# The recurrence's products, sums and last ratio on another engine, and its keys turned one slice later

## The reference, cut to what matters

```python
x = x + tanh(g_ffn[0])   * ffn0(layernorm(x), W_up, W_gate, W_down)      # silu(up) * gate, 2048 wide
x = x + tanh(g_xattn[1]) * wkv(w, u, k=layernorm(x), v=ctx)

def step(carry, kv_t):                # wkv, scanned over the 256 positions, per channel
    p, q, o = carry
    kt, vt = kv_t
    no = maximum(o, u + kt)
    A = exp(o - no)
    E = exp(u + kt - no)
    y = (A * p + E * vt) / (A * q + E)
    no2 = maximum(w + o, kt)
    A2 = exp(w + o - no2)
    E2 = exp(kt - no2)
    return (A2 * p + E2 * vt, A2 * q + E2, no2), y
```

## Time and profile before

| | |
|---|---|
| median of 3 runs | 3439.24 us (3435.51 to 3440.72) |
| the profiled execution, first to last instruction | 3438.0 us |
| the same beside the median of the runs | 1.2 us less |
| mean granted TensorE clock | 0.944 |
| a pass of the stage (passes 3 to 6) | 53.5 us |
| the stage, from its first matmul to the last L856 | 403.4 to 879.5 us |

### The profile page before, as it was taken

The page is one execution under the profiler, slowest core; times in us unless marked ns, Lnnn a source line. Parts: engine busy times, 40 slices in busy tenths (PEclk is TensorE's granted clock), DMA queues, the critical chain, the costliest instruction groups (busy, mean ns, idle before and its releaser), DMA issues.

```text
span 3438.0 us, 50056 instructions
## 1 busy us (share of the span) xinstructions
PE 2938.0 (85%) x18354; PEld 1708.0 (50%) x18354; DVE 2538.5 (74%) x4602; ACT 1663.7 (48%) x2597; POOL 955.8 (28%) x1357
## 2 busy tenths in 40 slices
PE   4999898884689899677788747999999999988998
PEld 2344566663344444355666523455555455544665
DVE  5699669999766666688888878777777777766333
ACT  3000144444345555248889974444454444455433
POOL 2566100000300000025767775222222222211000
PEclk7999999997799999899899968999999999999999
DMA  7233111212211011110000021000000000021000
GB/s 266 81 92 92 41 56 61 62 50 73 57 26 32 23 26 47 53 38 7 1 1 2 9 93 55 1 7 7 1 7 7 1 7 7 1 65 37 13 18 18
DMA packets 52643, 132.51 MB, mean 39 GB/s; under 512 B 6416, under 2 KB 19536, under 8 KB 51152
## 3 DMA queue, kind: packets, MB, share of 16 engines
q1 hardware_dynamic: 43216, 96.11, 9.2%
q10 hardware_dynamic: 9216, 33.56, 3.2%
HBM read 119.03 MB, written 4.19 MB: 36 GB/s over the span
## 4 chain that ended last, share of the span: by engine, by line
PE 50%; DVE 24%; issue 12%; ACT 10%; POOL 3%; DMA 1%; DVEq 0%; SPq 0%; POOLq 0%; ACTq 0%
PE psum L1106 10%; PE psum L517 8%; ACT area_g L2149 4%; PE psum L2074 4%; PE psum L2604 3%; PE psum L2563 3%; PE psum L668 3%; PE psum L2588 2%; PE psum L2573 2%; PE psum L1955 2%; DVE area_a L1713 2%; PE psum L2095 2%; PE psum L1361 2%; PE psum L1342 2%; DVE xn L2861 1%
## 5 line engine op out<-in xcount | busy, mean ns | idle before, releaser
L2149 ACT ACTIVATE area_g<-area_a 128x2048 bf16<-128x2048 f32 x168 | 334.7, 1997 | 33.3 <-POOL area_a L2018 24.0
L2074 PE MATMUL psum<-area_c,ident_bf 128*128 128x128 bf16 x3328 | 231.1, 234 | 97.6 <-DVE area_c L2183 97.5
L172 POOL TENSOR_TENSOR rstd<-mean_var,eps_col 128x2 f32<-128x2 f32 x65 | 21.3, 327 | 1048.3 <-DVE mean_var L590 565.0
L517 PE MATMUL psum<-area_b,area_g 128*128 128x512 f32 x640 | 279.1, 599 | 3.9 <-DVE x_stream L455 2.4
L2074 PEld LDWEIGHTS psum<-area_c,ident_bf 128*128 128x128 bf16 x3328 | 216.2, 106 | 122.9 <-DVE area_c L2183 116.0
L2563 PE MATMUL psum<-area_b,stage 128*128 128x512 f32 (+1 forms) x512 | 237.4, 546 | 0.0
L668 PE MATMUL psum<-xT_high,area_a 128*128 128x256 f16 x1024 | 235.2, 278 | 1.4 <-DVE xT_low L605 1.4
L668 PE MATMUL psum<-xT_low,area_a 128*128 128x256 f16 x1024 | 234.9, 279 | 0.0
L2854 DVE TENSOR_REDUCE small<-psum 128x1 f32<-128x384 f32 (+1 forms) x256 | 158.4, 619 | 70.4 <-PE psum L2564 68.3
L2715 ACT ACTIVATE xn<-psum,small 128x384 f32<-128x384 f32 (+1 forms) x256 | 163.8, 640 | 96.1 <-DVE small L2854 95.9
L2480 POOL TENSOR_TENSOR small<-small,half_pow 128x4 f32<-128x4 f32 x96 | 131.7, 1371 | 273.9 <-DVE small L2801 273.9
(11 more groups left out here) (412 smaller groups left out, 7645.3 us busy)
## 6 DMA issues: line engine op xcount, KB each, us to landing
stage<-in_w ACTq DMA_DIRECT2D x24, 512.0 KB, 4.4
stage<-in_w SPq DMA_DIRECT2D x24, 512.0 KB, 3.6
area_g<-in_toeplitz SPq DMA_DIRECT2D x32, 256.0 KB, 2.6
area_b<-in_ctxT SPq DMA_DIRECT2D x15, 512.0 KB, 3.8
area_b<-area_b SPq DMA_DIRECT2D x24, 256.0 KB, 3.7
stage<-in_ctxT SPq DMA_DIRECT2D x9, 512.0 KB, 3.9
x_stream<-in_x SPq DMA_DIRECT2D x4, 1024.0 KB, 9.0
area_c<-in_ctxT SPq DMA_DIRECT2D x4, 1024.0 KB, 15.7
```

Of the source, the lines that this page charges most:

```text
L517: last = nc.tensor.matmul(psum[:, 4 * par + m, :], toep[:, par, (m - k) * P:(m - k + 1) * P], kv[:, par, k, :], start=(k == 0), stop=(k == m))
L2074: last = nc.tensor.matmul(psum[:, 1, t_ * P:(t_ + 1) * P], identb[:, :], above5[:, t_, c * P:(c + 1) * P], start=(c == 0), stop=(c == KE - 1))
L2149: nc.scalar.activation(junk5[t_], z5[b % 3][:, t_, :], ACT.Sign, bias=fine5[:, par, t_:t_ + 1], scale=-1.0, accum_out=signs5[:, t_:t_ + 1] ...
```

## The change

- `products`, `totals` and `ratio` leave VectorE. On GpSimd three functions take their place: `denominator(c)` (a product and a sum), `numerator(c)` (two products and a sum) and `ratio(c)` (a product). In pass b, GpSimd does the rstd for the keys of element b-1, `denominator(b-2)`, the rstd for the next feed-forward front, `numerator(b-2)` and `ratio(b-2)`.
- For the last element VectorE keeps the denominator and the ratio (`last_denominator`, `last_ratio`), GpSimd makes the numerator.
- The reciprocal of the first half waits for the denominator alone; each reciprocal now counts up a semaphore, for which GpSimd's ratio waits. `weights_scan` waits for the numerator before it overwrites `wk_ev`.
- The two turns of the keys move from slices 1 and 2 to slices 2 and 3, on TensorE and on ScalarE.

```diff
+            def denominator(c):
+                if c < 0:
+                    return
+                pool.wait_ge(sig("wkv_exp_ready"), 2 * c + 2)
+                pool.wait_ge(sig("wkv_pq_ready"), KD * (c + 1))
+                if c:
+                    pool.wait_ge(sig("wkv_y_ready"), c)
+                pc.link(nc.gpsimd.tensor_tensor(wk_den, wk_d[:, 0], wk_q[:, :, 0:S], ALU.mult))
+                nc.gpsimd.tensor_tensor(wk_den, wk_den, wk_d[:, 1], ALU.add).then_inc(sig("wkv_den_ready"), 1)
+
+            def numerator(c):
...
+                pc.step(nc.gpsimd.tensor_tensor(wk_num, wk_d[:, 0], wk_p[:, :, 0:S], ALU.mult))
+                nc.gpsimd.tensor_tensor(wk_ev, wk_d[:, 1], wk_v, ALU.mult).then_inc(sig("wkv_ev_ready"), 1)
+                pc.settle()
+                pool.wait_ge(sig("wkv_ev_ready"), 2 * c + 2)
+                nc.gpsimd.tensor_tensor(wk_num, wk_num, wk_ev, ALU.add).then_inc(sig("wkv_den_ready"), 1)
+
+            def ratio(c):
+                if c < 0:
+                    return
+                pool.wait_ge(sig("wkv_inverted"), 2 * c + 2)
+                pool.wait_ge(sig("wkv_den_ready"), 2 * c + 2)
+                if c:
+                    pool.wait_ge(sig("wkv_yT_ready"), TT * c)
+                nc.gpsimd.tensor_tensor(wk_y, wk_num, wk_den, ALU.mult).then_inc(sig("wkv_y_ready"), 1)
+
             rstd_of(front_of_ffn(0))
             for b in range(B + 2):
                 if 1 <= b <= B:
                     rstd_of(front_of_wkv(b - 1))
+                    denominator(b - 2)
                 if b + 1 < B:
                     rstd_of(front_of_ffn(b + 1))
+                if 1 <= b <= B:
+                    numerator(b - 2)
+                    ratio(b - 2)
                 if b == B:
                     rstd_of(NEXT)
                     rstd_of(NEXT + 1)
+            numerator(B - 1)
...
-                    if j == 1:
-                        keys(b - 1, 0)
                     if j == 2:
                         y_back(b - 3, 1)
-                        keys(b - 1, 1)
+                    if j in (2, 3):
+                        keys(b - 1, j - 2)
...
-                    if j in (1, 2):
-                        key_copy(b - 1, j - 1)
+                    if j in (2, 3):
+                        key_copy(b - 1, j - 2)
...
+            def last_denominator(c):
                 dve.wait_ge(sig("wkv_exp_ready"), 2 * c + 2)
                 dve.wait_ge(sig("wkv_pq_ready"), KD * (c + 1))
-                dc.settle()
-                dc.step(nc.vector.tensor_tensor(wk_den, wk_d[:, 0], wk_q[:, :, 0:S], ALU.mult))
-                dc.step(nc.vector.tensor_tensor(wk_num, wk_d[:, 0], wk_p[:, :, 0:S], ALU.mult))
-                nc.vector.tensor_tensor(wk_ev, wk_d[:, 1], wk_v, ALU.mult).then_inc(sig("wkv_ev_ready"), 1)
...
+                dve.wait_ge(sig("wkv_y_ready"), c)
+                dc.link(nc.vector.tensor_tensor(wk_den, wk_d[:, 0], wk_q[:, :, 0:S], ALU.mult))
+                dc.link(nc.vector.tensor_tensor(wk_den, wk_den, wk_d[:, 1], ALU.add))
+                dve.sem_inc(sig("wkv_den_ready"), 1)
...
@@ -907,10 +935,6 @@
-                    if j == 1:
-                        products(b - 2)
-                    if j == 2:
-                        totals(b - 2)
                     if j == 3:
                         invert(b - 2, 0)
...
                     if j == 6:
                         invert(b - 2, 1)
-                    if j == 7:
-                        ratio(b - 2)
```

More of the change, by code:

```diff
@@ L818, in dve_stage12 @@
                 dc.step(nc.vector.memset(z[:, :, 0:1], v))
-            def products(c):
-                if c < 0:
-                    return
+            def last_denominator(c):
                 dve.wait_ge(sig("wkv_exp_ready"), 2 * c + 2)
                 dve.wait_ge(sig("wkv_pq_ready"), KD * (c + 1))
-                dc.settle()
-                dc.step(nc.vector.tensor_tensor(wk_den, wk_d[:, 0], wk_q[:, :, 0:S], ALU.mult))
-                dc.step(nc.vector.tensor_tensor(wk_num, wk_d[:, 0], wk_p[:, :, 0:S], ALU.mult))
-                nc.vector.tensor_tensor(wk_ev, wk_d[:, 1], wk_v, ALU.mult).then_inc(sig("wkv_ev_ready"), 1)
[L830 to L836, removed]
+                dve.wait_ge(sig("wkv_y_ready"), c)
+                dc.link(nc.vector.tensor_tensor(wk_den, wk_d[:, 0], wk_q[:, :, 0:S], ALU.mult))
+                dc.link(nc.vector.tensor_tensor(wk_den, wk_den, wk_d[:, 1], ALU.add))
+                dve.sem_inc(sig("wkv_den_ready"), 1)
             def invert(c, half):
@@ L840, in invert, with last_ratio @@
                     return
-                dve.wait_ge(sig("wkv_den_ready"), 2 * c + 2)
[L842 to L848, removed]
+                if c < B - 1:
+                    dve.wait_ge(sig("wkv_den_ready"), 2 * c + 1)
+                part_ = wk_den[:, 2 * half:2 * half + 2, :]
+                nc.vector.reciprocal(part_, part_).then_inc(sig("wkv_inverted"), 1)
+            def last_ratio(c):
+                dve.wait_ge(sig("wkv_inverted"), 2 * c + 2)
+                dve.wait_ge(sig("wkv_den_ready"), 2 * c + 2)
                 nc.vector.tensor_tensor(wk_y, wk_num, wk_den, ALU.mult).then_inc(sig("wkv_y_ready"), 1)
@@ L883, in weights_scan @@
                 dve.wait_ge(sig("wkv_v_loaded"), 16 * (c + 1))
+                if c:
+                    dve.wait_ge(sig("wkv_den_ready"), 2 * c)
                 nc.vector.tensor_tensor(wk_ev, wk_d[:, 3], wk_v, ALU.mult).then_inc(sig("wkv_ev_ready"), 1)
@@ L950, in dve_stage12 @@
             norm_apply(dve, front_of_wkv(c), c)
-            products(c - 1)
             add_y(c - 2, 0)
-            totals(c - 1)
             add_y(c - 2, 1)
@@ L959, in dve_stage12 @@
             invert(c - 1, 1)
-            ratio(c - 1)
             dve.wait_ge(sig("wkv_added"), TT + TT * (c - 1))
@@ L970, in dve_stage12 @@
             sums34(dve, dc)
-            products(c)
-            totals(c)
+            last_denominator(c)
             squares_to_pool(dve, dc)
@@ L976, in dve_stage12 @@
             invert(c, 1)
-            ratio(c)
+            last_ratio(c)
             for t_ in range(TT):
```

## The result

The changed kernel takes 3467.85 us (median of 4 runs, 3466.23 to 3469.77), the kernel before 3439.82 beside it: a ratio of 1.0083, 95% interval 1.0068 to 1.0097. It is slower by 28.0 us; 3463 was forecast.

A forecast was written before the change was run, and what follows sets the result against it. The bound was VectorE's order in the code, with the points where TensorE needs something from it. Passes 18.6 plus tail 4.9 gave 23.5 us, the span going from 3438.0 to 3461.5; median 3463, range 3443 to 3480.

The forecast's parts named there:

- The hold of L595: Pass 5, slice 0: GpSimd's product starts 0.07 us before L595 and holds it; the pair takes some 5 us, not 1.0.
- Rivals B and E: B: VectorE wins the race after L173, 3450, chance 0.2; E: product starts after L595, about 3438, chance 0.12.
- Rival C: Only L595 is held, while L925 and the scans go free: +17.6 us, 3457, chance 0.05.
- Two of the signs named: In the trace, L925 of slice 3 and L865 would be stretched; no size given.
- The sum: Whole span: 18.6 us from the passes plus 4.9 from the tail, 23.5 us slower.
- the half clock: TensorE's clock at 0.50 for 3 us after its stop, making the way to slice 3's matmuls 1.5 us longer.
- The size of GpSimd's operations: Each 128x1024 operation on GpSimd was taken at 2.35 us, range 2.1 to 2.75.
- Pass 5, term by term: Addition L856 +1.5 us, slow clock +1.5, slice 3 2.95 late, L925 waiting 0.3 for the numerator: +3.3 us.
- Pass 7, the term that was mis-sized: No next pass's front, so the numerator comes earlier; +2.9 us from slice 3 and 0.4 for transposes: +3.3.
- Pass 1, pass 2, the tail: Pass 1 -2.0 us, TensorE's wait for keys gone; pass 2 +4.1, norm_apply meeting the numerator; tail +4.9, scans held.
- Rival D: No hold counts, and what leaves VectorE leaves the path: -19 us, 3420, chance 0.11.
- The later keys: TensorE's slice-2 products only come earlier, then it stands nearly 8 us with a slow clock after; pass 1 gains 2.0.

The follow-up runs named there:

- e3: The changed kernel with one more wait: GpSimd waits before each denominator until both L595 of the keys' front are done; 3438.2 us.
- e6: The kernel before with two GpSimd operations of 128x1012 on spare SBUF, read by nothing, added behind the keys' rstd in passes 1 to 7; 3461.6 us.
- e2: The changed kernel with the turns of the keys back in slices 1 and 2; 3467.4 us.
- e11: The changed kernel with the denominator in full on GpSimd, numerator and ratio cut to 2 of 256 positions; 3448.4 us.
- e4: The changed kernel with all GpSimd products, sums and ratios of the recurrence cut to 2 of 256 positions, waits and orders kept; 3420.1 us.
- e1: The kernel before with only the keys turned one slice later, the recurrence staying on VectorE; 3449.9 us.

## Why the prediction was right

**The direction and the mechanism.** The hold of L595 by a product that follows L173 at once was the main step, and it is as it was written: 0.07 us ahead, L595 4.87 us long (about 5 was named as the sign). e3 and e6 show it from both sides. Rivals B and E (VectorE wins the race, or the product starts after L595) occurred in none of passes 2 to 7 nor in the tail. Rival C (only L595 is held) is out: L947 took 2.87 us in pass 7, L948 2.56 in e2, the four scans 5.32 in the tail, all with two inputs in SBUF. The Trainium skill's page "SBUF — State Buffer", section Who interferes with whom, says that a VectorE instruction with two SBUF inputs contends with a GpSimd instruction that reads SBUF, and the trace agrees. Two of the signs named did not come: in passes 3 to 6 neither L925 (now L947) of slice 3 nor L865 (now L891) is stretched; the scans of L865 are so in the tail alone.

**The sum.** 23.5 us were added up; the same stretches measured 27.0. That hides larger errors: passes 2, 4, 5 and 7 came 5.8 us above the forecast together, passes 1, 3, 6 and the tail 2.3 under it. The terms that matter in this are the half clock and pass 7.

**The size of GpSimd's operations.** Taken at 2.35 us; measured 2.17 for L643 and L653, 2.36 for L654 and L657, 2.40 for L644 with the short hold in it, and 2.67 for the ratio L666, which starts while L947 runs.

**Pass 5, term by term.** Slice 3 was to start 2.95 us late, and L925 to wait 0.3 for the numerator: +3.3. It started 4.2 late (22.17 us after slice 0's L931, 17.97 before), and L947 waited for nothing (0.63). Both differences are one term, the half clock, which was taken as 3 us long and lasted 6. The addition came 1.25 us late instead of 1.5. The two transpose groups behind it were as forecast, the down products took 3.4 us instead of 2.35, and from slice 3's first matmul to its L931 went 4.2 us instead of 3.8. L931 came late enough to miss the numerator.

**Passes 3 to 6, the half clock.** These passes differ from the kernel before by +2.7 to +4.2 us, and from the start of slice 3 on all are alike, so the difference lies ahead of it. The stop of TensorE is 7.70 us in each. What differs is how long the clock stays at 0.50 behind it. The six us behind the stop in passes 3, 4 and 6 (pass 5 has 0.50 in all six), then three us behind the 3.08 us stop in pass 4 of the kernel before:

```profile
569.00:575.00 6.00, 5.99 (x30) 4.06 (x31) 3.51 (x7) 2.24 (x5) 1.32 (x3) 0.67 0.39 128
625.60:631.60 6.00, 5.95 (x23) 3.63 (x24) 3.51 (x7) 2.28 (x5) 1.29 (x3) 0.55 0.44 144
740.60:746.60 6.00, 5.97 (x34) 4.35 (x35) 3.51 (x7) 2.27 (x5) 1.30 (x3) 0.75 0.42 125
...
611.85:614.85 3.00, 3.00 (x27) 2.74 (x28) 2.96 (x5) 1.25 (x3) 0.00 (x0) 1.00 0.12 15
```

A mean of 0.67, 0.55, 0.50 and 0.75 over six us is, with the two levels 0.50 and 1.00, about 4.0, 5.4, 6.0 and 3.0 us at half clock. Work at half clock takes twice as long, so half of each length is lost. That, plus the 1.25 us by which the addition is late, is 3.3, 4.0, 4.3 and 2.8 us, within 0.1 of the measured differences of passes 3, 4, 5 and 6. (The lengths at half clock are worked out from the means and not read.) So the step from hold to pass length is right in every pass, and the forecast's 3 us of half clock is what pass 6 alone had. In the kernel before, pass 4 has the same stop as pass 5 and no half clock at all: one pass read for a term was not enough.

**Pass 7, the term that was mis-sized.** The prediction has "the numerator comes earlier; +2.9 from slice 3": its sum has no hold of slice 1's L925 by the numerator. L947 lost to the numerator's second product by 0.02 us (795.31 to 795.33), so the addition and TensorE's second turn came another 2.2 us late. The half clock behind TensorE's stop lasted 6 us here too and cost 1.4 us more than forecast. Together: +6.8 instead of +3.3. e11, without the numerator's length, has 55.6, so 2.3 of the 6.8 are the numerator's.

**Pass 1, pass 2, the tail.** -2.3 for -2.0; +4.9 for +4.1; +3.6 for +4.9. In pass 2 the numerator holds as described and slice 4 starts 3.5 us late; TensorE stands 4.4 us for the held L595 pair there, with the clock at 0.50 behind, and slice 5 is another 1.4 us late, which the sum did not have. The tail's scans behaved as described, but scans and differences together end 3.3 us late instead of 3.9. Up to the state scan L886 it is 2.8 for 3.6, and element 7 adds 0.8 for 1.3.

**Rival D, measured.** e4 is its world. It came at 3420.1, where 3420 was written, but partly by luck: pass 2 (48.2: -3.4 for -3.3) and the tail (-7.8 for -7.7) fit, the passes 3 to 6 gave 0.4 us each on average instead of 1.3 and pass 7 lost 0.5, and 3.7 us came from outside the stage. Where the gain of passes 3 to 6 goes can be read: the addition does come 2.6 us earlier, and the half clock behind a stop of 3.8 us takes 1.5 to 2.9 of it back, against the 1.5 forecast. That stop comes with the later keys; what the offload without holds would give with the keys in their old places was not run. e3, which only lets L595 through first, is level with the kernel before.

**The later keys.** The prediction said that they buy nothing in passes 3 to 6 and bring the slow clock. e1 shows that they cost 9.3 us alone. What wasn't seen is that with the keys early slice 3 runs into the numerator's hold (e2), so that in the changed kernel the later keys cost nothing.

## What to carry to other kernels

Moving an elementwise operation from VectorE to GpSimd is not a removal. Here, while a GpSimd product ran, L595 and the VectorE instructions with two SBUF inputs waited for its end (4.87 us for 1.00, 2.87 for 0.69). So look at what VectorE issues next, and do not start a long GpSimd operation right behind a short one that VectorE waits for. One wait on the right semaphore was worth 30 us here. Before moving work, look for the instruction that the other engine stands for. An addition put into a gap of 0.86 us, with the keys a slice later, and a group of matmuls put in front of a waiting one gave 22.9 us; taking six operations off VectorE gave 20.5 even where GpSimd's part was cut to almost nothing (e4). And a stop of TensorE costs twice, by its length and by the clock behind it, and the second part varies from pass to pass.

## What the runs showed of the hardware that was not expected

The length of a stop does not tell how long TensorE's clock stays low behind it. In the kernel before the granted clock was 0.50 for 3 us after a stop of 3.08 us in pass 5, and 1.00 after the same stop in pass 4; in the changed one it was 0.50 for about 3.0 to 6.0 us after four stops of 7.70 us. I had sized it by one row. What sets the length no run here shows. And the race between the two engines is decided by hundredths: starts 0.07 us (L643 and L595) and 0.02 us (L654 and L947 in pass 7) ahead held the later one for about 2.2 us.
